# Attention and a mixture of experts on one core: probabilities times values of a query tile in one run

## The chip, the cores and the metric

The kernel runs on one core of one Trainium2 chip. The metric is the time of one execution on the device, in microseconds. The changed kernel is compared with the kernel before on the same inputs.

## The reference

One layer over 2048 tokens of 128 values, in float32. It is causal attention with 8 heads of 64, then a layer norm, a mixture of 16 experts (top 2) with a shared expert, and a second layer norm. The change touches the attention alone:

```
t = tokens * rsqrt(mean(tokens * tokens) + eps) * rms_w
q, k, v = einsum('bnd,hde->bhne', t, wq / wk / wv)
score = where(causal_mask, -max, einsum('bhie,bhje->bhij', q, k) * scale)
out = einsum('bhij,bhje->bhie', softmax(score), v) * sigmoid(t @ w_gates)
pred = einsum('bhne,hed->bnd', out, wo)
x = layernorm(tokens + pred)
```

## The kernel before

The 8 heads are worked on in 4 pairs, the first three in a loop, the last one outside of it. Each engine has its own queue, written by hand, and they wait for each other by semaphores. Within a pair the 2048 queries are 16 tiles of 128, in the order 0, 2, ..., 14, 15, 13, ..., 1 (`ORDER`), and s is the place in that order. The keys of tile t are the key tiles 0 to t, cut into chunks of 512 keys, four key tiles each (`chunks[s]`), of which the last may be narrower.

A query tile goes through four stages, each a step later than the one before:

- `scores` (step s): per head and chunk, TensorE multiplies into one of four PSUM banks ps_s (L1044, L1048 for the mask, L1050). VectorE copies the bank into probs, with the maximum of each row (L755), and after the last chunk reduces the maxima (L761, L762). ScalarE then takes the exponential of the whole row of the head at once, in place (`exps`, L557).
- `turn` (step s + 1): per head and chunk, TensorE transposes the up to four 128x128 blocks into ps_t (L961). There are two such banks, taken in turn by the number g of the group. Groups with an even g are moved to probsT by ScalarE (L568), those with an odd g by VectorE (L771); the moves raise moved0 and moved1. Group g waits until group g - 2 is moved.
- `times_v` (step s + 2): TensorE multiplies the transposed probabilities by v_sb, key tile by key tile and head by head, and adds up in ps_o (L1079): 128x64 weights, 128 columns. In the trace each float32 matmul has two records, so a key tile has four. ScalarE then unloads ps_o into outT (`unload`, L578).
- `times_wo` (step s + 3): TensorE multiplies by the output weights (L1089), and VectorE adds the result to x_acc (L780 to L787), which raises acc_done.

Which unit comes when is set once for all engines by `step_units(s, project)`. Each stage of a step is a list of units. Unit i of a list of n gets the key (i + 0.5) / n, for times_v (i + 0.7) / n, and the units of the step are sorted by it. Before, times_v has one unit per chunk of the tile, so up to four in a step. An engine works its units off in that order; a unit whose wait isn't met holds those behind it.

After the four pairs come the layer norm, the shared expert, the routing and the 16 experts. The change touches none of them.

Of the kernel before, what the change touches and what calls it, by code (L numbers as in the profile page):

```python
# [5 lines left out]
def attention_moe_layer(nc, tokens, wq, wk, wv, wo, w_gates, rms_w, Wg, W1, b1, W11, b11, W2, b2,  # L6
# [12 lines left out]
    P = 128  # L19
# [7 lines left out]
    BT = BANK // P  # L27
# [27 lines left out]
    first = {}  # L55
# [16 lines left out]
    n0, n1, n2, n3 = NORM_ORDER  # L72
    norm_at = {NT: [("stats", n0), ("stats", n1)], NT + 1: [("norm", n0), ("norm", n1), ("stats", n2)]}

    def step_units(s, project):

        units = []
        if s < NT:
            units += [("scores", s, h, c, w) for h in range(2) for c, w in chunks[s]]
        stages = [units]  # L80
        if 1 <= s <= NT:
            stages.append([("turn", s - 1, h, c, w) for h in range(2) for c, w in chunks[s - 1]])
        if 2 <= s < NT + 2:
            stages.append([("times_v", s - 2, 0, c, w) for c, w in chunks[s - 2]])
        if s >= 3:
            stages.append([("times_wo", s - 3, 0, 0, 0)])
        if project:
            stages.append([("project", w, 0, c, 0) for w, c in project_at.get(s, [])])
        else:
            stages.append([(stage, 0, 0, c, 0) for stage, c in norm_at.get(s, [])])  # L90
        placed = [((i + (0.7 if x[0] == "times_v" else 0.5)) / len(u), k, x) for k, u in enumerate(stages) for i, x in enumerate(u)]
        return [x for _, _, x in sorted(placed, key=lambda y: y[:2])]
# [24 lines left out]
    with ctx:  # L117
# [385 lines left out]
        def _(act):  # L503
# [48 lines left out]
            def pair(p, units, fill_of):  # L552
                def exps(s, h):
                    w = (ORDER[s] + 1) * P
                    row = slice(2 * s + h, 2 * s + h + 1)
                    act.wait_ge(row_max, p * (2 * NT) + (2 * s + h + 1))
                    nc.scalar.activation(probs[s % 2][h][:, 0:w], probs[s % 2][h][:, 0:w], ACT.Exp,  # L557
                                         bias=nmax[:, row], scale=SCALE,
                                         accum_out=rsum[:, row]).then_inc(exp_done, 1)

                def move(s, h, c, w):
                    g = first[s, h] + c
                    if g % 2 == 0:
                        if s >= 2:

                            act.wait_ge(pv_done, p * NT + (ONE + s - 1))
                        act.wait_ge(turned, p * GROUPS + (ONE + g + 1))
                        nc.scalar.activation(  # L568
                            probsT[s % 2][h][:, c * BT:c * BT + w // P, :].rearrange("p n i -> p (n i)"),
                            ps_t[0][:, 0:w], ACT.Copy).then_inc(moved0, 1)  # L570

                def unload(s):
                    act.wait_ge(pv_done, p * NT + (ONE + s + 1))

                    act.wait_ge(wo_done, p * NT + (ONE + max(s - 1, 0)))
                    for h in range(2):
                        rows = slice(h * DH, (h + 1) * DH)
                        nc.scalar.activation(outT[s % 2][h][rows, :], ps_o[s % 2][rows, 0:P], ACT.Copy).then_inc(out_ready, 1)  # L578

                for x in units:  # L580
                    stage, s, h, c, w = x
                    if stage == "project":
                        project(x, fill_of[x], p * FILLS + (PROJECTIONS + fill_of[x]), p)
                    elif stage == "scores" and (c, w) == chunks[s][-1]:
                        exps(s, h)
                    elif stage == "turn":
                        move(s, h, c, w)
                    elif stage == "times_v" and (c, w) == chunks[s][-1]:
                        unload(s)
                    elif stage in ("stats", "norm", "turn_x"):  # L590
                        norm(stage, c)
# [367 lines left out]
        def _(pe):  # L959
# [67 lines left out]
            def pair(p, units, fill_of):  # L1027
                def free_bank(n):

                    if n < RING:  # L1030
                        pe.wait_ge(v_ready, p * NC + (n + 1))
                    else:
                        pe.wait_ge(freed, p * FREED + (ONE + KQ_FILLS + n - RING + 1))

                def scores(s, h, c, w, n):
                    t = ORDER[s]
                    if s == 0 and h == 0:

                        pe.wait_ge(freed, p * FREED + (ONE + KQ_FILLS))

                        pe.wait_ge(k_twice, p * (64 * NC) + 64 * NC)
                    free_bank(n)
                    q = q_hl[h][:, t * P:(t + 1) * P]
                    nc.tensor.matmul(ps_s[n % RING][:, 0:w], q, k_h[h][:, c * BANK:c * BANK + w],  # L1044
                                     start=True, stop=False)
                    if c == len(chunks[s]) - 1:

                        nc.tensor.matmul(ps_s[n % RING][:, w - P:w], ident_b[:, :], mask_b[:, :],  # L1048
                                         start=False, stop=False, skip_group_check=True)
                    nc.tensor.matmul(ps_s[n % RING][:, 0:w], q, k_l[h][:, c * BANK:c * BANK + w],  # L1050
                                     start=False, stop=True).then_inc(fill, 1)

                def turn_probs(s, h, c, w):
                    g = first[s, h] + c
                    if c == 0:
                        pe.wait_ge(exp_done, p * (2 * NT) + (2 * s + h + 1))

                    pe.wait_ge((moved0, moved1)[g % 2], p * (GROUPS // 2) + (ONE + g // 2))
                    for j in range(w // P):
                        at = c * BANK + j * P  # L1060
                        mm = turn(ps_t[g % 2][:, j * P:(j + 1) * P], probs[s % 2][h][:, at:at + P])
                    mm.then_inc(turned, 1)

                def times_v(s, c, w):
                    t = ORDER[s]
                    if c == 0:
                        if s == 0:

                            pe.wait_ge(v_ready, p * NC + NC)

                        pe.wait_ge(acc_done, p * NT + (ONE + max(s - 1, 0)))

                    done = first[s, 1] + c + 1
                    pe.wait_ge(moved0, p * (GROUPS // 2) + (ONE + (done + 1) // 2))
                    pe.wait_ge(moved1, p * (GROUPS // 2) + (ONE + done // 2))
                    for j in range(c * BT, c * BT + w // P):
                        for h in range(2):
                            rows = slice(h * DH, (h + 1) * DH)
                            mm = nc.tensor.matmul(ps_o[s % 2][rows, 0:P], v_sb[:, j, rows], probsT[s % 2][h][:, j, :],  # L1079
                                                  start=(j == 0), stop=(j == t))  # L1080
                    if j == t:
                        mm.then_inc(pv_done, 1)

                def times_wo(s):
                    pe.wait_ge(out_ready, p * (2 * NT) + (ONE + 2 * s + 2))
                    if s == 0:
                        pe.wait_ge(pair_wo, p + 1)
                    for h in range(2):
                        mm = nc.tensor.matmul(ps_o[s % 2][:, P + h * D:P + (h + 1) * D], outT[s % 2][h][:, :], wo_p[:, :],  # L1089
                                              start=True, stop=True)  # L1090
                    mm.then_inc(wo_done, 1)

                for x in units:
                    stage, s, h, c, w = x
                    if stage == "project":
                        if high_of.get(x) == 0:

                            pe.wait_ge(pair_w, p * 2 + 2)
                        free_bank(fill_of[x])
                        project(x, fill_of[x], p + 1)  # L1100
                    elif stage == "scores":
                        scores(s, h, c, w, fill_of[x])
                    elif stage == "turn":
                        turn_probs(s, h, c, w)
                    elif stage == "times_v":
                        times_v(s, c, w)
                    elif stage == "times_wo":
                        times_wo(s)
                    elif stage == "turn_x":
                        norm(stage, c)  # L1110
# [127 lines left out]
```

## Time and profile before

| | |
|---|---|
| device time, 3 runs | 773.39 us median, 773.01 to 776.36 |
| profiled execution: span from the first to the last instruction | 773.9 us |
| the profiled execution's own time | no separate number; the span is 0.5 us above the median |
| attention, four pairs | from 34.3 to 566 us of the span |
| TensorE matmul row busy | 688.3 us (89%) |
| VectorE, ScalarE, GpSimd busy | 534.2 us (69%), 419.2 us (54%), 105.3 us (14%) |
| mean granted TensorE clock | 0.947 |

Times are microseconds of one profiled execution. PE is TensorE's matmul row and PEld its weight loads, DVE is VectorE, ACT is ScalarE. The ends of matmuls are modelled and overlap; the distance between starts tells how fast they follow each other.

### The profile page before, as it was taken

How to read it: one execution, taken by the hardware profiler on the slowest of the kernel's cores; microseconds unless marked ns; L12 is line 12 of the kernel's file. 1: busy time of each engine (PE TensorE's matmuls, PEld its weight loads, DVE VectorE, ACT ScalarE, POOL GpSimd, SP SyncE). 2: the span in 40 equal slices, each digit the busy share in tenths (PEclk: the TensorE clock that was granted, in tenths of full speed). 3: DMA queues.
4: the chain of work that ended last, by engine and by line, in shares of the span. 5: the costliest groups of instructions: out<-in, count | busy, mean ns of one | idle time of the engine just before them, and what ended most of it. 6: DMA issues, size and time to landing. Idle time of an engine off the chain costs nothing.

```text
span 773.9 us, 17695 instructions
## 1 busy us (share of the span) xinstructions
PE 688.3 (89%) x5442; PEld 523.0 (68%) x5443; DVE 534.2 (69%) x1874; ACT 419.2 (54%) x908; POOL 105.3 (14%) x172
## 2 busy tenths in 40 slices
PE   4799999979999997999999899999958987999940
PEld 3577777747777774777777577777744556878830
DVE  4687767678777777787767888776787523556536
ACT  4766555656655557655555766554533213454445
POOL 2000000000000000000000000000021773565540
PEclk9999999998999999899999999999976996999975
DMA  8300000040000004000000694000090112222224
GB/s 188 83 2 1 2 3 1 8 107 2 1 2 2 2 1 111 3 1 1 2 2 1 145 130 4 2 2 2 1 302 25 49 52 56 65 63 64 67 73 113
DMA packets 56260, 33.64 MB, mean 43 GB/s; under 512 B 23776, under 2 KB 49520, under 8 KB 56176
## 3 DMA queue, kind: packets, MB, share of 16 engines
q1 hardware_dynamic: 53616, 27.33, 17.6%
q0 software_dynamic: 2560, 5.26, 2.0%
q8 instruction: 44, 0.72, 0.4%
q14 instruction: 40, 0.33, 0.1%
HBM read 14.70 MB, written 9.48 MB: 31 GB/s over the span
## 4 chain that ended last, share of the span: by engine, by line
PE 61%; issue 12%; DVE 12%; POOL 6%; ACT 4%; DMA 3%; SPq 0%; POOLq 0%; DVEq 0%; ACTq 0%
PE ps_o L1079 16%; PE ps_t L961 16%; PE ps_s L1044 9%; PE ps_s L1050 8%; POOL x_sorted L480 4%; PE ps_o L1089 3%; PE ps_s L1193 3%; DVE q_hl L674 2%; PE ps_o L1208 2%; DMA y_rows<-y_sb,row_now 1%; DVE k_l L674 1%; ACT probsT L568 1%; PE ps_s L1048 1%; DVE probs L755 1%; POOL y_rows L490 1%
## 5 line engine op out<-in xcount | busy, mean ns | idle before, releaser
L755 DVE TENSOR_SCALAR_CACHE_REDUCE probs<-ps_s 128x512 f32<-128x512 f32 (+3 forms) x320 | 192.1, 607 | 77.2 <-PE ps_s L1050 75.2
L557 ACT ACTIVATE probs<-probs,nmax 128x128 f32<-128x128 f32 (+15 forms) x128 | 154.0, 1203 | 133.5 <-DVE nmax L762 133.1
L961 PE MATMUL ps_t<-ident,probs 128*128 128x128 f32 x1104 | 181.6, 281 | 17.5 <-ACT probs L529 11.1
L961 PEld LDWEIGHTS ps_t<-ident,probs 128*128 128x128 f32 x1104 | 130.8, 142 | 64.7 <-issue 23.5
L1079 PE MATMUL ps_o<-probsT,v_sb 128*64 128x128 f32 x2176 | 154.4, 280 | 0.0
L1044 PE MATMUL ps_s<-k_h,q_hl 128*128 128x512 f32 (+3 forms) x320 | 145.2, 454 | 6.1 <-issue 5.4
L1079 PEld LDWEIGHTS ps_o<-probsT,v_sb 128*64 128x64 f32 x2176 | 115.7, 137 | 38.6 <-issue 36.1
L1050 PE MATMUL ps_s<-k_l,q_hl 128*128 128x512 f32 (+3 forms) x320 | 128.5, 402 | 0.0
L568 ACT ACTIVATE probsT<-ps_t 128x512 f32<-128x512 f32 (+3 forms) x160 | 89.6, 560 | 62.2 <-PE ps_t L961 60.8
L771 DVE COPY probsT<-ps_t 128x512 f32<-128x512 f32 (+3 forms) x160 | 91.1, 570 | 25.7 <-PE ps_t L961 25.3
L1044 PEld LDWEIGHTS ps_s<-k_h,q_hl 128*128 128x128 f32 x320 | 62.4, 195 | 19.3 <-issue 14.8
L1050 PEld LDWEIGHTS ps_s<-k_l,q_hl 128*128 128x128 f32 x320 | 64.2, 201 | 0.0
L430 POOL COPY wo_p<-wo_sb 128x128 f32 (+1 forms) x4 | 1.2, 293 | 408.1 <-PE ps_o L1089 399.3
L1193 PE MATMUL ps_s<-xgT,w_now 128*128 128x128 f32 x384 | 54.9, 288 | 1.1 <-ACT xgT L617 0.2
L490 POOL DMA_INDIRECT y_rows<-y_sb,row_now x48 | 47.3, 984 | 45.2 <-POOL row_now L486 37.7
L1193 PEld LDWEIGHTS ps_s<-xgT,w_now 128*128 128x128 f32 x384 | 48.3, 198 | 6.5 <-issue 4.4
L922 DVE SCALAR_TENSOR_TENSOR hid<-ps_s,b_col,sil 128x128 f32<-128x128 f32 x96 | 29.2, 346 | 32.1 <-ACT sil L622 26.7
L1089 PE MATMUL ps_o<-wo_p,outT 128*128 128x128 f32 x256 | 41.1, 284 | 6.4 <-ACT outT L578 6.4
L1089 PEld LDWEIGHTS ps_o<-wo_p,outT 128*128 128x128 f32 x256 | 34.7, 194 | 11.5 <-ACT outT L578 7.1
L629 ACT ACTIVATE y_sb<-ps_o 128x128 f32<-128x128 f32 x48 | 13.3, 277 | 50.9 <-DMA y_rows<-y_sb,row_now 47.7
L972 PE MATMUL ps_s<-tT,wkq_p 128*128 128x512 f32 x64 | 35.6, 667 | 2.4 <-DVE tT L696 1.7
L578 ACT ACTIVATE outT<-ps_o 64x128 f32<-64x128 f32 x128 | 34.1, 267 | 5.2 <-PE ps_o L1079 3.4
(150 smaller groups left out, 790.3 us busy)
## 6 DMA issues: line engine op xcount, KB each, us to landing
k_h<-k_h SPq DMA_DIRECT2D x32, 128.0 KB, 2.3
k_l<-k_l SPq DMA_DIRECT2D x32, 128.0 KB, 2.4
w_up<-in_L_ffn_W SPq DMA_DIRECT2D x2, 2048.0 KB, 12.1
xg<-x_sorted SPq DMA_DIRECT2D x48, 64.5 KB, 1.8
x_sorted<-zeros SPq DMA_DIRECT2D x12, 256.0 KB, 9.5
act_s<-y_rows SPq DMA_DIRECT2D x8, 256.0 KB, 4.9
x_acc<-in_L_attn_tokens SPq DMA_DIRECT2D x4, 256.0 KB, 3.6
out<-x_acc SPq DMA_DIRECT2D x4, 256.0 KB, 2.3
```

The source lines that it names most:

```text
L490: nc.gpsimd.indirect_dma_start(out=y_rows, out_offset=bass.IndirectOffsetOnAxis(ap=row_now[:, b:b + 1], axis=0), in_=y_sb[:, b, :], in_off ...
L557: nc.scalar.activation(probs[s % 2][h][:, 0:w], probs[s % 2][h][:, 0:w], ACT.Exp, bias=nmax[:, row], scale=SCALE, accum_out=rsum[:, row]). ...
L568: nc.scalar.activation(probsT[s % 2][h][:, c * BT:c * BT + w // P, :].rearrange("p n i -> p (n i)"), ps_t[0][:, 0:w], ACT.Copy).then_inc(m ...
L755: nc.vector.tensor_scalar(probs[s % 2][h][:, c * BANK:c * BANK + w], ps_s[n % RING][:, 0:w], 1.0, None, ALU.mult, ALU.max, accum_out=cmax[ ...
L771: nc.vector.tensor_copy(probsT[s % 2][h][:, c * BT:c * BT + w // P, :].rearrange("p n i -> p (n i)"), ps_t[1][:, 0:w]).then_inc(moved1, 1)
L961: return nc.tensor.transpose(dst, src, ident[:, :])
L972: mm = nc.tensor.matmul(ps_s[n % RING][:, :], wkq_p[:, w, :], tT[:, c * BANK:(c + 1) * BANK], start=True, stop=True)
L1044: nc.tensor.matmul(ps_s[n % RING][:, 0:w], q, k_h[h][:, c * BANK:c * BANK + w], start=True, stop=False)
L1050: nc.tensor.matmul(ps_s[n % RING][:, 0:w], q, k_l[h][:, c * BANK:c * BANK + w], start=False, stop=True).then_inc(fill, 1)
L1079: mm = nc.tensor.matmul(ps_o[s % 2][rows, 0:P], v_sb[:, j, rows], probsT[s % 2][h][:, j, :], start=(j == 0), stop=(j == t))
L1089: mm = nc.tensor.matmul(ps_o[s % 2][:, P + h * D:P + (h + 1) * D], outT[s % 2][h][:, :], wo_p[:, :], start=True, stop=True)
L1193: mm = nc.tensor.matmul(ps_s[2 * b + a][:, m * P:(m + 1) * P], w_now[:, b, a * H + m * P:a * H + (m + 1) * P], xgT[:, b, :], start=True, s ...
```

## The change

The list of times_v units of a tile has one entry, with all its chunks, where it had one entry per chunk. With one unit, the key of the spread-out order is 0.7 in each step. On TensorE, times_v goes over all key tiles 0 to t in one go. It waits at its start for all moves of the tile, where each unit waited for those of its chunk. ScalarE unloads at the place of the single unit. Work, data, buffers and DMAs are the same.

```diff
+    def pv_groups(s):
+
+        return [(0, len(chunks[s]))]
+
     def step_units(s, project):
...
         if 2 <= s < NT + 2:
-            stages.append([("times_v", s - 2, 0, c, w) for c, w in chunks[s - 2]])
+            stages.append([("times_v", s - 2, 0, c, w) for c, w in pv_groups(s - 2)])
...
-                    elif stage == "times_v" and (c, w) == chunks[s][-1]:
+                    elif stage == "times_v" and (c, w) == pv_groups(s)[-1]:
                         unload(s)
...
-                def times_v(s, c, w):
+                def times_v(s, c, end):
                     t = ORDER[s]
...
-                    done = first[s, 1] + c + 1
+                    done = first[s, 1] + end
                     pe.wait_ge(moved0, p * (GROUPS // 2) + (ONE + (done + 1) // 2))
                     pe.wait_ge(moved1, p * (GROUPS // 2) + (ONE + done // 2))
-                    for j in range(c * BT, c * BT + w // P):
+                    for j in range(c * BT, min(end * BT, t + 1)):
```

## Rows read from the trace of the kernel before

**Rows 1.** The page: busy tenths and granted clock in 40 equal slices of the span.
```profile
PE   4799999979999997999999899999958987999940
...
DVE  4687767678777777787767888776787523556536
...
PEclk9999999998999999899999999999976996999975
```

**Rows 2.** Windows: us; PE, PEld, DVE, ACT, POOL busy (instructions), PEclk, DMA share, GB/s.
```profile
34.30:171.20 136.90, 130.12 (x1120) 98.50 (x1120) 103.36 (x344) 82.15 (x156) 0.85 (x4) 1.00 0.08 17
...
sum 531.70, PE 512.18 PEld 390.48 DVE 401.24 ACT 318.09 POOL 1.97; mean PE 128.04 PEld 97.62 DVE 100.31 ACT 79.52 POOL 0.49
```

**Rows 3.** Timeline, 90 to 96 us: start, duration, engine, operation [idle before <-releaser].
```profile
89.79 0.69 DVE L771 COPY probsT<-ps_t 128x512 f32<-128x512 f32 x1
...
90.39 0.68 DVE L755 TENSOR_SCALAR_CACHE_REDUCE probs<-ps_s 128x512 f32<-128x512 f32 x1
90.41 0.44 PE L1079 MATMUL ps_o<-probsT,v_sb 128*64 128x128 f32 x4
...
90.78 0.49 PE L1044 MATMUL ps_s<-k_h,q_hl 128*128 128x512 f32 x1
...
91.00 0.08 DVE L755 DVE_READ_ACCUMULATOR probs<-ps_s 128x1 f32 x1
...
91.47 0.49 PE L961 MATMUL ps_t<-ident,probs 128*128 128x128 f32 x3
...
91.72 0.48 PE L1044 MATMUL ps_s<-k_h,q_hl 128*128 128x512 f32 x1
...
92.26 0.60 PE L961 MATMUL ps_t<-ident,probs 128*128 128x128 f32 x4
...
92.78 2.00 ACT L557 ACTIVATE probs<-probs,nmax 128x2048 f32<-128x2048 f32 x1 [1.22 <-DVE nmax L762]
...
92.79 1.09 PE L1079 MATMUL ps_o<-probsT,v_sb 128*64 128x128 f32 x16
...
93.81 0.50 PE L1044 MATMUL ps_s<-k_h,q_hl 128*128 128x512 f32 x1
...
94.39 0.60 PE L961 MATMUL ps_t<-ident,probs 128*128 128x128 f32 x4
...
94.74 0.48 PE L1044 MATMUL ps_s<-k_h,q_hl 128*128 128x512 f32 x1
...
94.90 0.60 ACT L568 ACTIVATE probsT<-ps_t 128x512 f32<-128x512 f32 x1
...
95.55 0.66 PE L961 MATMUL ps_t<-ident,probs 128*128 128x128 f32 x4
```

**Rows 4.** Timeline of PE, 80 to 112 us: a run of 12 and the next unit.
```profile
102.54 0.88 PE L1079 MATMUL ps_o<-probsT,v_sb 128*64 128x128 f32 x12
103.35 0.39 PE L1044 MATMUL ps_s<-k_h,q_hl 128*128 128x256 f32 x1
```

**Rows 5.** Waits over the span: who <- for whom: us in total, times, longest.
```profile
PEld ps_o L1079 <- issue: 36.1, 142, 0.8
...
PEld ps_t L961 <- ACT probsT L568: 17.2, 32, 1.2
```

**Rows 6.** Timeline, 47.5 to 57.9 us.
```profile
50.88 0.31 PE L1044 MATMUL ps_s<-k_h,q_hl 128*128 128x128 f32 x1
...
54.28 0.60 ACT L568 ACTIVATE probsT<-ps_t 128x512 f32<-128x512 f32 x1
...
56.37 0.48 PE L1044 MATMUL ps_s<-k_h,q_hl 128*128 128x512 f32 x1
...
57.73 0.33 PE L961 MATMUL ps_t<-ident,probs 128*128 128x128 f32 x1 [0.65 <-ACT probsT L568]
```

**Rows 7.** Timeline of PE at the start of the second pair.
```profile
171.26 0.32 PE L1044 MATMUL ps_s<-k_h,q_hl 128*128 128x128 f32 x1 [2.75 <-issue]
```

**Rows 8.** Windows at the start of the second pair.
```profile
174.00:180.00 6.00, 6.00 (x27) 4.47 (x27) 3.89 (x18) 3.53 (x10) 0.00 (x0) 0.57 0.00 1
```

## The prediction, made before the changed kernel was run

> **What bounds the kernel now.** I read the page first, then the windows of the four head pairs, the order of TensorE's work in a middle step, the list of waits, and the chain behind the longest stall. TensorE's matmul row is busy for 89% of the span, VectorE for 69%, and the granted clock shows 9 tenths nearly everywhere [rows 1]. In the four stretches of attention, together 531.7 us, TensorE is busy for 512.2 us and VectorE for 401.2 us [rows 2]. So in attention TensorE's queue sets the time. A microsecond taken from its stream is gained only if the next instruction isn't then held by ScalarE or VectorE.
>
> **What a run of probabilities times values costs.** A key tile of 128 takes 4 matmul records (two heads, two records each). In [rows 3] I compare start times. A run of 16 records starts 0.53 us after the four transposes before it (92.26 to 92.79), where a score unit starts 0.35 us after such transposes (94.39 to 94.74): 0.18 us is lost on the way in. The next unit starts 1.02 us after a run of 16 and 0.37 us after a run of 4 (90.41 to 90.78), and 0.81 us after one of 12 [rows 4]. That is (1.02 - 0.37) / 12 = 0.054 us a record and 0.155 us beside the records. So each run costs 0.34 us whatever its length, where it stands between transposes and scores (0.32 us between scores and transposes, by the same reading). The waits agree: the weight load of these runs sat idle before 142 of them, 36.1 us in all, with nothing that released it [rows 5].
>
> **What the change removes.** The tile order is 0, 2, ... 14, 15, 13, ... 1. A tile t has t // 4 + 1 runs before and one after, so a pair goes from 4 x (1 + 2 + 3 + 4) = 40 runs to 16. 24 runs x 4 pairs = 96, and 96 x 0.33 = **31.7 us** less on TensorE. The matmuls, their data and the number of turn, score and output units stay. The waits on moved0 and moved1 that the longer run asks for at its start were met a step before: its tile was turned in the previous step. The wait on acc_done is later than before and so free. The semaphore waits that go are inside the 0.33 us. No DMA changes, and GpSimd only waits for wo_done. Bounds of the saving: 24 us, from 36.1 / 142 = 0.25 us a run [rows 5], and 35 us, from 0.36 us a run where the following unit is also slow by 0.02 us.
>
> **What the change moves.** Several units with one fractional key spread over the step: runs stood at 0.175, 0.425, 0.675 and 0.925 of a step. The single one stands at 0.7. So the first 0.7 of a step holds no such run, and the last 0.3 holds up to 64 records, 64 x 0.054 + 0.34 = 3.8 us. What did the runs in the first part hide? The chain is in [rows 3] too: at 90.78 the last score unit of the second head starts, VectorE copies it and takes the maximum, at 92.78 ScalarE starts the exponential of the whole row (2.00 us), and only then, at 94.90, it moves the first turned group of the next step (0.60 us) out of ps_t0. The second group after that needs the same bank, so TensorE can start it only at 95.55: 4.77 us after 90.78. Between lies its own work: masked scores 0.69, transposes of 3 tiles 0.25, scores 0.55, transposes with the way into a run 0.53, **the run 1.02**, scores 0.57, transposes 0.35, scores 0.55, together 4.51. The stall is 0.26 us. After the change the run isn't there: the work is 4.51 - 1.20 = 3.31 and the stall is 4.77 - 3.31 = 1.46 us. The whole run, not only its fixed part, turns into waiting.
>
> I did this sum for each row's second head in a pair: the delay from the last score unit to the end of the first move, read from the traces of the two engines (the first and the longest of the ten, s = 4 and s = 8, are in [rows 3, 6]), plus 0.05 us, less the work that the new order leaves. With step s as place in the tile order (s = 8 is tile 15), delay / work left / stall in us:
> s = 4: 4.05 / 2.70 / 1.35; s = 5: 4.00 / 2.97 / 1.03; s = 6: 3.98 / 2.67 / 1.31; s = 7: 4.43 / 2.97 / 1.46; s = 8: 4.77 / 3.30 / 1.47; s = 9: 4.07 / 2.62 / 1.45; s = 10: 4.32 / 3.15 / 1.17; s = 11: 3.62 / 2.75 / 0.87; s = 12: 3.89 / 3.59 / 0.30; s = 13: 3.19 / 2.51 / 0.68.
> That is 11.1 us a pair. The stalls of the same kind there now add up to 1.9 us a pair; of these the largest, 0.81 us before the transpose at 57.73 (scores at 56.37 take 0.55 us of the 1.36 between the two, [rows 6]; s = 5, first head), goes away, for after the first head's last scores the order now has the long run. The list of waits has 17.2 us in 32 such waits [rows 5], which with some 0.2 us each for a weight load that would have started early anyway is the same amount. At the other places (s = 0 to 3 and 14, 15) the order is the same or the cover suffices. Added: 9.2 x 4 = **36.8 us**.
>
> Two of the delays should shrink. In s = 4 and 6 VectorE was behind when the last, narrow score unit came; after the long run it has caught up. From its instructions (0.61 us a 512-wide score copy, 90.39 to 91.00, and 0.60 us a move, 89.79 to 90.39, [rows 3]) I take 0.2 and 0.25 us off, 1.8 us in four pairs. Against that, transposes that come after a stall or a run take 0.06 us longer to give way, for their weights were not loaded ahead (a difference that I read between the transposes after stalls and the others: 0.59 us to the next run where 0.53 is usual): about 1 us. Added in all: 36.
>
> **Is VectorE then the bound?** A new pair has 16 x 0.34 + 544 records x 0.054 = 34.8 us in long runs. The first pair's 137 us [rows 2] become 137 - 8 + 9 = 138, so 103 us lie between the runs. VectorE has 103.4 us busy in a pair, in 344 instructions, and some 0.03 us between each two: 114 us. So it has to do 11 us of its work inside the runs, 0.7 us in each. It can: when a run starts, it may be behind by a score copy or two and a move, 1.2 to 1.8 us. I add nothing, but the margin is thin, and it makes rival B.
>
> **The sum.** The profiled execution's span is 773.9 us, 0.5 above the median of 773.39. 773.9 - 31.7 + 36 = 778.2, so **778 us** as a median: a change that takes 96 switches off TensorE and gives the same time back as waits for ScalarE.
>
> **The rivals.**
> *A, the saving wins.* The exponential's cover isn't as short as I add up, because TensorE's stall lets VectorE run ahead and the row maximum comes 0.3 us earlier everywhere. Ten stalls x 4 pairs x 0.3 = 12 us less: 766 us. With no new stall at all, 773.9 - 31.7 = 742 us. Against it: the stalls of now sit where this sum puts them, with 0.1 us of error. Chance 0.20.
> *B, VectorE becomes the bound.* It idles in the long run, and what it was behind holds the turn banks or the score banks between the runs. If it did nothing in any run, a pair would take 114 + 34.8 = 149 us instead of 138: 4 x 11 = 44 us more, 822. It decides from where the lag at a run's start falls under the 0.7 us that it needs. If it is three quarters of that, a quarter of the bound is lost: 11 us, 789. Against it: four score banks and two turn banks let TensorE be ahead by more than that. Chance 0.20, with 783 to 800. A rule of the Trainium skill speaks for this side: "Perfetto Trace Analysis", section "Optimization Strategy", advises interleaving stretches that are bound by different engines, which is what the old order does and the new one undoes. By that rule the new order is slower, as in B; this case's trace bears it out so far as the stall without a run is longer by the run.
> *C, the clock falls.* Before 171.26 TensorE had idled for 2.75 us [rows 7], and from 174 to 180 us the granted clock is 0.57, so most of that time at the lower of its two levels, 1.2 of 2.4 GHz [rows 8]: 6 x 0.43 = 2.6 us lost. The point from which it decides: if stalls of 1 us or more are enough, there are seven in each pair, 28 x 2.6 = 73 us, 851 us. Against it: the stall of 0.81 us at 57.73 did not lower it, and between two stalls lie some 10 us of full work. Chance 0.05.
> *D, the change doesn't save what it removes*, because a long run stalls in itself where the short ones ended: 773.9 + 36 = 810 us with nothing saved, 798 with a third. Nothing inside the runs of 16 shows it. Chance 0.03.
>
> **How the numbers follow.** Forecast 0.52, with its own range of 771 to 785 (saving 24 to 35, stalls 32 to 40). The range that should hold it 8 times in 10: from A's 766 to B's 789. A measurement of this kernel tells 0.5%, 3.9 us, from no change; so faster is under 769.5 and slower over 777.3. Of the forecast's 0.52, 0.20 lies above, 0.30 within and 0.02 below. A gives 0.16 faster and 0.04 the same; B, C and D 0.27 slower with 0.01 the same. Together: faster 0.18, same 0.35, slower 0.47.
>
> **What would show it.** 16 runs a pair with 0.054 us a record inside and the weight load's idle time before them down from 36 to some 14 us. Idle time of the transposes for ScalarE's move up from some 20 to 45 to 55 us, in stalls of 0.7 to 1.5 us, once a step, on the second even group. VectorE's waits for scores longer, up to 3 us, once a step, in the long run. The first-head stall at s = 5 gone. Wrong if the stall falls on another engine's wait (VectorE's move, the score banks), if a run's records slow down inside, or if the clock shows dips in the middle of pairs.

## The result: 0.5% slower, and the profile after

The changed kernel takes 777.74 us (median of 20 runs, 774.47 to 781.48), the kernel before in the same comparison 773.42 us (20 runs, 770.83 to 776.80). The ratio is 1.005, with a 95% interval of 1.0033 to 1.0066: 4.3 us slower, 2.6 to 5.1.

The profiled execution of the changed kernel has a span of 774.4 us and took 776.17 us. So some 1.8 us lie around a span, and the profiled execution of before (773.9 us) was about 2 us over its median. Differences between the two traces as wholes are therefore good to some 2 us. I compare the pairs of heads. The windows of the changed kernel, with the columns of [rows 2]:

```profile
32.26:170.40 138.14, 124.88 (x1120) 98.55 (x1121) 102.27 (x344) 81.93 (x157) 1.14 (x5) 1.00 0.08 17
170.40:309.24 138.84, 125.82 (x1121) 99.36 (x1121) 102.33 (x344) 81.70 (x156) 0.82 (x3) 0.98 0.08 17
309.24:445.38 136.14, 126.63 (x1120) 100.37 (x1121) 102.10 (x344) 81.20 (x155) 0.29 (x1) 0.98 0.11 24
```

The three looped pairs take 138.1, 138.8 and 136.1 us; before they took 136.9 [rows 2], 138.8 and 135.2. The fourth, from its first score unit to its last output matmul, takes 129.0 us for 127.7. TensorE is busy for 5 to 7 us less in each looped pair, and the time is the same or a little longer: 3.4 us in the four together. The granted clock of a pair is no lower than before (1.00, 0.98, 0.98 for 1.00, 0.97, 0.98). The second pair hides part of its loss in the clock. In the trace of before it was low for longer at that pair's start: 0.57 in the 6 us from 174 [rows 8], and 0.87 in the 6 us ahead of them:

```profile
168.00:174.00 6.00, 2.77 (x18) 1.97 (x16) 2.50 (x14) 1.58 (x5) 0.53 (x2) 0.87 0.04 11
```

In the changed kernel the same two stretches read:

```profile
168.00:174.00 6.00, 3.22 (x15) 2.44 (x16) 2.34 (x13) 1.87 (x8) 0.16 (x1) 0.78 0.03 8
174.00:180.00 6.00, 5.89 (x40) 4.34 (x38) 5.65 (x27) 4.52 (x12) 0.00 (x0) 0.93 0.01 1
```

By the granted clock that is 3.4 us lost before (6 x 0.13 + 6 x 0.43) and 1.7 us after, so at an equal clock this pair would be over 1 us longer as well.

The waits over the span (columns as in [rows 5]) show what took the place of the work:

```profile
DVE probs L759 <- PE ps_s L1054: 114.7, 99, 4.0
...
PEld ps_t L965 <- ACT probsT L572: 43.0, 46, 1.7
...
PE ps_t L965 <- ACT probsT L572: 27.4, 35, 1.2
...
PEld ps_o L1083 <- issue: 15.9, 53, 0.8
PEld ps_t L965 <- DVE probsT L775: 14.1, 40, 0.7
```

The idle time before the runs' weight loads went from 36.1 to 15.9 us, that of the transposes for ScalarE's move from 17.2 to 43.0 us [rows 5]. And a wait is there that the kernel before did not have, 14.1 us of transposes for VectorE's move. These are idle times of the weight loads, which otherwise run ahead of the matmuls, so TensorE itself loses less: by the starts of its units 34.7 us at the waits for ScalarE's move (10.0 before) and some 6.7 us at those for VectorE's. A long run and the unit after it (TensorE, 106 to 114 us):

```profile
109.08 3.71 PE L1083 MATMUL ps_o<-probsT,v_sb 128*64 128x128 f32 x64
112.72 0.50 PE L1048 MATMUL ps_s<-k_h,q_hl 128*128 128x512 f32 x1
```

The 64 records take 3.64 us from start to start, against 1.02 us for 16 [rows 3]: (3.64 - 1.02) / 48 = 0.055 us a record, with nothing lost inside. The stall of s = 8 in the timeline of the changed kernel, 88 to 98 us, answers to [rows 3]:

```profile
89.19 0.47 PE L1048 MATMUL ps_s<-k_h,q_hl 128*128 128x512 f32 x1
...
91.17 2.01 ACT L561 ACTIVATE probs<-probs,nmax 128x2048 f32<-128x2048 f32 x1 [1.10 <-DVE nmax L766]
...
92.10 0.48 PE L1048 MATMUL ps_s<-k_h,q_hl 128*128 128x512 f32 x1
...
93.17 0.58 ACT L572 ACTIVATE probsT<-ps_t 128x512 f32<-128x512 f32 x1
...
93.80 0.66 PE L965 MATMUL ps_t<-ident,probs 128*128 128x128 f32 x4 [0.98 <-ACT probsT L572]
```

From the last score unit of the second head to the freed transposes it is 93.80 - 89.19 = 4.61 us, where it was 4.77. TensorE used to fill all but 0.26 us of it; now the score unit at 92.10 (0.55 us) is the last thing that it has, and the excess is 1.15 us.

### The profile page after: what moved, and what is told of

Same layout as the page of the kernel before. It is cut to its first block, busy times and chain, and to the rows that moved or that the text cites. A ratio compares the mean times of both kernels' runs of the same rounds, so it can differ in the third digit from the quotient of the medians.

```text
span 774.4 us, 17599 instructions
## 1 busy us (share of the span) xinstructions
PE 663.6 (86%) x5442; PEld 521.6 (67%) x5443; DVE 528.8 (68%) x1874; ACT 417.3 (54%) x908; POOL 105.2 (14%) x172
## 4 chain that ended last, share of the span: by engine, by line
PE 49%; issue 18%; DVE 17%; ACT 7%; POOL 5%; DMA 3%; SPq 1%; DVEq 0%; POOLq 0%; ACTq 0%
PE ps_o L1083 16%; PE ps_t L965 11%; PE ps_s L1048 6%; PE ps_s L1054 5%; POOL x_sorted L484 4%; PE ps_s L1197 3%; ACT probsT L572 3%; DVE probs L759 3%; PE ps_o L1093 3%; DVE q_hl L678 2%; PE ps_o L1212 2%; DVE k_l L678 2%; DMA y_rows<-y_sb,row_now 2%; ACT probs L561 1%; DVE probsT L775 1%
## 5 line engine op out<-in xcount | busy, mean ns | idle before, releaser
L965 PE MATMUL ps_t<-ident,probs 128*128 128x128 f32 x1104 | 179.5, 280 | 42.1 <-ACT probsT L572 27.4
L1083 PE MATMUL ps_o<-probsT,v_sb 128*64 128x128 f32 x2176 | 132.9, 275 | 1.3 <-DVE probsT L775 1.3
L1083 PEld LDWEIGHTS ps_o<-probsT,v_sb 128*64 128x64 f32 x2176 | 117.6, 137 | 17.8 <-issue 15.9
L1093 PEld LDWEIGHTS ps_o<-wo_p,outT 128*128 128x128 f32 x256 | 34.7, 194 | 9.5 <-ACT outT L582 6.5
L484 POOL DMA_INDIRECT x_sorted<-rows,slot x32 | 32.1, 1004 | 25.3 <-DVE slot L867 15.8
```

Of the source, the lines that this page charges most:

```text
L484: nc.gpsimd.indirect_dma_start(out=x_sorted, out_offset=bass.IndirectOffsetOnAxis(ap=slot[:, k, t:t + 1], axis=0), in_=rows[:, k, t, :], i ...
L965: return nc.tensor.transpose(dst, src, ident[:, :])
```

## The experiments

The theory: a run costs 0.33 us of TensorE where it is entered and left, and each step loses the cover of ScalarE's late move. The rivals: the 0.33 us belong to the unit's semaphore waits; VectorE, starved in the long run, is what costs; the saving fills a hole that is there anyway. Ratios are to the kernel before, run on the same chip in turn.

**Four units, back to back.** The kernel before, with all units of a tile at one key:

```diff
-        placed = [((i + (0.7 if x[0] == "times_v" else 0.5)) / len(u), k, x) ...
+        placed = [(0.7 if x[0] == "times_v" else (i + 0.5) / len(u), k, x) ...
```

> The kernel before, with its one unit per 512 keys and all its waits, but all units of a tile with the key 0.7, so that they stand back to back where the changed kernel has its one run. Theory (the 0.33 us a run are paid where TensorE changes between the 64-column weights of these matmuls and the 128-column ones of the others; the loss is ScalarE's late move): the same time as the changed kernel, 777.7 us, within 2 us. Rival (the 0.33 us belong to a unit's own semaphore waits and end): 24 such ends a pair come back, 96 x 0.33 = 32 us more, 810 us; with the waits as half of it, 794 us.

777.01 us, ratio 1.0055 (1.0038 to 1.0072): the changed kernel's time. The waits at the ends of the units cost nothing that can be seen, within some 1.5 us. Its waits are those of the changed kernel:

```profile
PEld ps_t L961 <- ACT probsT L568: 43.6, 47, 1.7
...
PEld ps_o L1079 <- issue: 14.8, 50, 0.8
```

So what a run costs lies at the change to and from the other units, and the effect of the diff is that of the order; what the merged loop adds can't be seen. The Trainium skill, "TensorEngine Tiling (Array Packing)", section "Key Properties", says that changing the tiling mode drains TensorE. This case's trace has a loss at that change: 0.18 us into and 0.155 us out of the 128x64 matmuls, counted from the starts between scores and transposes, both 128x128. That it is a drain, and that the width is the reason, was not tested by itself.

**One run, early.** In the changed kernel:

```diff
+        placed = [(0.2 if x[0] == "times_v" else (i + 0.5) / len(u), k, x) ...
```

> The changed kernel with the key of the single run at 0.2 instead of 0.7 of its step. Theory (ScalarE's late move after the second head's exponential needs a run as cover): the run now stands in that gap, the second head's stalls go (11 us a pair by my sum), and stalls of the first head of 0.2 to 1.3 us come in its place, 7.0 us a pair in all; by the sum of the units a pair takes 2.7 us less than before the change: 773.4 - 11 = 762 us, 757 to 767. Rival (VectorE starves in the long run, wherever it stands): as the changed kernel, 776 to 780 us.

814.42 us, ratio 1.0529 (1.0506 to 1.0552): both sides missed. The waits show one that neither had, and TensorE's timeline where (two runs of short tiles):

```profile
PE ps_o L1083 <- DVE probsT L775: 37.4, 38, 2.6
```

```profile
147.50 1.97 PE L1083 MATMUL ps_o<-probsT,v_sb 128*64 128x128 f32 x32 [1.48 <-DVE probsT L775]
154.36 2.61 PE L1083 MATMUL ps_o<-probsT,v_sb 128*64 128x128 f32 x24 [2.04 <-DVE probsT L775]
```

A single run needs every move of its tile, and the last group is turned at the end of the step before. At 0.2 of a short step that move isn't done, and TensorE's queue stands, 1.48 and 2.04 us in the two rows. In the first pair ten runs wait, 10.0 us together; the pair takes 148.7 us (start to start of the pairs). Before the change the first unit at 0.175 needed only the first chunk's moves. The sum of cover said nothing of this, for it held only one kind of wait.

**Two runs.** Tiles with more than one chunk get two runs, one for each half of the chunks:

```diff
     def pv_groups(s):
-        return [(0, len(chunks[s]))]
+        n = len(chunks[s])
+        return [(0, 1)] if n == 1 else [(0, (n + 1) // 2), ((n + 1) // 2, n)]
...
+        placed = [((0.7 if len(u) == 1 else (0.2, 0.7)[i]) if x[0] == "times_v" else (i + 0.5) / len(u), k, x) ...
```

> The changed kernel with two runs per tile (the halves of its chunks; tiles with one chunk keep one run at 0.7) at the keys 0.2 and 0.7: 28 runs a pair instead of 16 or 40. Theory: 12 x 0.33 = 4 us a pair less than before the change on TensorE, and each half covers one of the two exponentials, so that stalls of 0.3 us a pair are left where the kernel before has 1.8 by the same sum: 5.4 us a pair, 773.4 - 22 = 752 us, 746 to 758. Rival (VectorE starves in long runs): half of the change's loss stays, so 773.4 - 16 + 18 = 775 us.

756.93 us, ratio 0.9781 (0.9758 to 0.9805): 16 to 17 us faster than the kernel before, 5 us short of the forecast of 752 and within its range. The pairs take 132.8, 134.1 and 130.7 us. The waits of the transposes, 36 to 540 us:

```profile
PEld ps_o L1084 <- issue: 25.3, 106, 0.8
...
PEld ps_t L966 <- DVE probsT L776: 8.1, 20, 0.6
...
PEld ps_t L966 <- ACT probsT L573: 7.4, 21, 0.7
```

The 43.0 us of waits for ScalarE's move are down to 7.4. The sum of the units gave 5.4 us a pair, the pairs show 4.1 to 4.7.

> Two runs per tile as before in this study, with the keys 0.25 and 0.65 instead of 0.2 and 0.7. Theory (the cover between exponential and the blocked transposes decides, and the sum of units gives both the same stalls within 0.1 us a pair): 757 us as with 0.2 and 0.7, within 4 us. Rival (the exact place matters through something the sum leaves out, as it did for the single runs at 0.2 and 0.95): off by more than 5 us.

With the keys 0.25 and 0.65: 755.91 us, ratio 0.9777 (0.9740 to 0.9815). Between these two pairs of keys the exact place does not matter. Either version beats both kernels.

**A short exponential.** In the changed kernel and in the one before, the exponential takes the last 128 columns of a row; the other columns stay raw scores and the row's sum is that of the 128:

```diff
-                    nc.scalar.activation(probs[s % 2][h][:, 0:w], probs[s % 2][h][:, 0:w], ACT.Exp,
+                    nc.scalar.activation(probs[s % 2][h][:, w - P:w], probs[s % 2][h][:, w - P:w], ACT.Exp,
```

> The changed kernel with the exponential of a row taken over its last 128 columns alone; the other columns go on as raw scores, and the sum of the row is that of the 128. So ScalarE's instruction takes 0.4 us instead of up to 2.0. Theory (the stall is the length of that instruction): the stalls on ScalarE's move, 9 us a pair in the changed kernel's trace, are gone, about 1 us at a pair's start too: 777.7 - 40 = 738 us, 733 to 745. Rival (VectorE is the bound between the runs): it hardly gains, 765 to 775 us, and the waits of the transposes turn to VectorE's move.

742.52 us, ratio 0.9612 (0.9591 to 0.9634).

> The kernel before, with the exponential of a row over its last 128 columns alone, as in the changed kernel's short-exponential run. Theory: it had only 2 to 3 us a pair of such stalls to lose, so 773 - 8 = 765 us, 760 to 768; and with the stalls gone from both, the distance to the changed kernel with the same edit (742.5) is what the 96 runs cost: 22 to 32 us. Rival (the single place starves VectorE and so costs for itself): the two short-exponential kernels are within 10 us of each other.

760.76 us, ratio 0.9824 (0.9795 to 0.9854). The edit takes 35 us from the changed kernel and 12 to 14 from the one before: the wait for the exponential's end is what the change put in. With it out of both, the fewer runs show a gain, 0.0212 of 773 = 16 us (18 by the medians), less than the 22 to 32 that I expected, and more than the rival's 10. The waits of the changed kernel with the short exponential show what else the change put in:

```profile
PEld ps_t L965 <- DVE probsT L775: 14.1, 40, 0.7
```

It is the same 14.1 us as with the full exponential, so it doesn't come from ScalarE's late move. By the starts of TensorE's units it holds TensorE for 6.7 us here as in the changed kernel. With that the 96 runs come to 23 to 25 us, 0.24 to 0.26 us each. That VectorE falls behind TensorE's denser stream between the runs is likely; no run here tests it.

**One run at 0.8**, the same edit of the key:

> The changed kernel with the key of the single run at 0.8 instead of 0.7, which puts it behind one more score unit. Theory (count of the cover between each exponential and the next transposes of its bank): the second head's stalls stay, and three of the first head's come in addition (s = 5, 11 and 12, 1.0 to 1.3 us, where the run now stands behind the blocked transposes): 3.5 us a pair, 777.5 + 14 = 791 us, 785 to 796. Rival (VectorE's idling in the long run is what costs, wherever it stands): 777 us.

783.85 us, ratio 1.0122 (1.0090 to 1.0153): slower than the changed kernel by some 6 us, and under the expected range of 785 to 796. The direction is the theory's, against a rival that had no change; the size is less than half of its 14 us. The waits show the stalls themselves:

```profile
PEld ps_t L965 <- ACT probsT L572: 54.4, 58, 1.8
```

That is 12 waits more than in the changed kernel, three a pair as expected. In the first pair they hold TensorE for 0.50, 0.39 and 0.86 us, where the sum had 1.0 to 1.3 each.

**One run at 0.95:**

> The changed kernel with the key of the single run at 0.95, the end of its step. The early run at 0.2 lost 10 us a pair in waits for the last move of its own tile, which the step before had only just turned; at 0.95 that move is a step old. Theory: the run covers the second head's exponential, the first head's stalls of 0.3 to 1.3 us come instead (6.7 us a pair by my sum), a pair takes 3.2 us less than before the change: 773 - 13 = 760 us, 755 to 766. Rival (a long run costs through VectorE wherever it stands): 775 to 780 us, or over 800 if the early run's 814 was due to the place in front of the second head's stall.

771.75 us, ratio 0.9967 (0.9951 to 0.9984). Faster than the changed kernel, as the theory has it and the rival hasn't, but 12 us short of the 760 and outside the expected 755 to 766. Reading the starts of units, the first pair's stalls are 0.88 and 0.90 us for the first heads of s = 7 and 8 (0.86 and 0.90 by the sum), but also 1.18 us at s = 4 and 1.0 us before an output unit, which the sum had at nothing: the late run puts off ScalarE's unload, for which the output unit waits and which at s = 4 stands between the exponential and the move.

**Runs of two key tiles.** 72 runs a pair:

```diff
-        return [(0, len(chunks[s]))]
+        n = ORDER[s] + 1
+        return [(j, min(j + 2, n)) for j in range(0, n, 2)]
...
-                    done = first[s, 1] + end
+                    done = first[s, 1] + (end + BT - 1) // BT
...
-                    for j in range(c * BT, min(end * BT, t + 1)):
+                    for j in range(c, end):
```

> The other way round: a run of probabilities times values for every two key tiles, 72 runs a pair instead of 40 or 16, spread over the step as before. Theory (0.33 us a run at the change of the weights' width): 32 x 0.33 = 11 us a pair more, less up to 1.8 us of stalls that the finer spread covers: 773 + 37 to 44 = 810 to 817 us. Rival (the idle time before these weight loads only fills a hole that is there anyway): 775 us.

806.61 us, ratio 1.0401 (1.0368 to 1.0433): 31 us more. There are 128 more units than before, but three in each pair stand right behind another (12 stretches of 16 records in the trace), so TensorE's stream has 276 runs where it had 160. 31 us for 116 runs are 0.27 us each after what the finer spread gained. The stalls on ScalarE's move that it took away were about 7 us in the kernel before, which makes up to 0.33 us a run. The runs cost TensorE time; they fill no hole. The time is 3 us under the expected 810 to 817, which was added up for 128 runs.

**A short accumulation.** The two additions into x_acc take one column instead of 128 (the others are left as they were). VectorE's busy time falls from 528.8 to 512.2 us in the changed kernel, 17 us where I had put it at 26:

```diff
-                        out=x_acc[:, t, :], in0=ps_o[s % 2][:, P:P + D], ...
+                        out=x_acc[:, t, 0:1], in0=ps_o[s % 2][:, P:P + 1], ...
```

> The changed kernel, with the two additions of a step into x_acc over one column instead of 128 (the other columns are left as they were), which takes some 0.4 us of VectorE's work out of each of 64 steps, 26 us in all. Theory (ScalarE's late move is the loss; VectorE has a thin margin): a few of the transposes' new waits on VectorE's move go, 3 to 4 us in attention; the stalls on ScalarE's move stay: 774 us, 770 to 777. Rival (VectorE is the bound between the runs): most of the 26 us come back, 755 to 765 us.

775.18 us, ratio 1.0024 (1.0008 to 1.0040).

> The kernel before with the same edit, for comparison. Theory: VectorE holds nothing there but the two 0.8 us stalls at which the accumulation stands before the score copy: 771 us, 768 to 774. The difference between the two kernels with this edit says how much of the change's loss is VectorE's: none if it stays near 4 us.

771.37 us, ratio 0.9965 (0.9944 to 0.9986). Less work for VectorE is worth 2 to 3 us in either kernel, and the distance between them stays: 3.8 us by the medians, 4.3 with the full accumulation. The time of the changed kernel is the expected one, but not for the expected reason. Its transposes' waits on VectorE's move, of which a few should have gone, are all there:

```profile
PEld ps_t L965 <- DVE probsT L775: 14.1, 40, 0.7
```

What the change loses, it doesn't lose to the accumulations. Whether less work on VectorE between the runs, score copies or moves, would shorten these waits was not tested.

## Why the prediction was right, step by step

The forecast of 778 us and its mechanism held: 96 entries fewer on TensorE, and about the same time back, most of it in waits for ScalarE's move. That the difference of 4.3 us (36 less 31.7) came out to the tenth is luck: the stalls were smaller than added up, VectorE's waits came on top, and the saving is known only as 23 to 32 us.

- **The cost inside a run and at its ends.** Inside, 0.055 us a record was measured for 0.054. The 0.18 and 0.155 us at the ends stand in the new trace as before. As a price in the kernel's time, a run was worth 0.24 to 0.26 us (short exponential) or 0.27 to 0.33 us (runs of two tiles) where I took 0.33. The saving is thus 23 to 32 us, where I predicted 31.7 with bounds of 24 and 35.
- **The stalls.** They are where the sum put them, one a step after the second head's last scores. In the second pair the excess over a unit's usual length, for s = 4 to 13, is 1.08, 0.90, 1.40, 1.30, 1.15, 0.81, 0.96, 0.24, 0 and 0.33 us, against 1.35, 1.03, 1.31, 1.46, 1.47, 1.45, 1.17, 0.87, 0.30 and 0.68. Together 8.2 us for 11.1, with 1.5 us beside them in waits for VectorE's move. Added to the kernel: (9.7 - 1.9) x 4 = 31 us for 36. Two things make the stalls smaller. The delay from the last score unit to the end of the move is 0.13 to 0.29 us shorter than I took it at eight of the ten steps (4.61 for 4.77 at s = 8); taking something off for s = 4 and 6 alone was wrong, and at s = 6 it didn't shrink (4.05 for 3.98). And TensorE takes longer over the work in between than I counted, for part of it waits for VectorE's move. At s = 9 the stretch from the last scores (240.40) to the freed transposes (244.32) holds these rows:

```profile
241.75 0.48 PE L1048 MATMUL ps_s<-k_h,q_hl 128*128 128x512 f32 x1
...
242.55 0.66 PE L965 MATMUL ps_t<-ident,probs 128*128 128x128 f32 x4
242.96 0.48 PE L1048 MATMUL ps_s<-k_h,q_hl 128*128 128x512 f32 x1
...
244.32 0.66 PE L965 MATMUL ps_t<-ident,probs 128*128 128x128 f32 x4 [0.64 <-ACT probsT L572]
```

The score unit at 241.75 takes 0.80 us to the next transposes instead of 0.55, because their bank waits for VectorE: 0.25 us of the stall only changed its name. The stall at the first head of s = 5 is gone, as said.
- **The run's own wait.** I said that its moves were met a step before. In the changed kernel this cost little, 1.3 us of matmul idle time in all; the early run at 0.2 shows that it depends on the place.
- **The balance.** 31 less 23 to 32 gives -1 to 8 us; the four pairs show 3.4 us in the traces, the runs 4.3 us. The rest is within what two traces can tell. My start of 773.9 us was a span and the result a time of the device, which is 1.8 us more; that execution was also 2 us slower than usual, so the mixture put the start only 0.5 us too high.
- **Rival A**, cover longer than counted, is true in part: the stalls are 0.3 us shorter on average, of which 0.13 us by an earlier exponential. It is not enough against the stalls that stay. **Rival B**, VectorE the bound, isn't what happened in the main: ScalarE's waits hold TensorE for 25 us more than before, VectorE's for 6.7 us, and the short accumulation closes none of the gap. But its wait exists, 14.1 us of weight-load idle time in 40 places where I "add nothing". Its 6.7 us are more than the 4.3 us of loss; but without it part of them would come back in longer waits for ScalarE, as the row of s = 9 shows. The rule of the Trainium skill ("Perfetto Trace Analysis", "Optimization Strategy": interleave stretches with different bounds) has the sign right, 1.005; but one piece for each exponential is enough, where the kernel before has one for each 512 keys: the two runs show it with 0.978. **Rival C**, the clock, didn't come: 0.98 to 1.00 in the pairs, with stalls up to 1.4 us. **Rival D** neither: nothing stalls inside 64 records.

## What to carry to other kernels

Work that costs something to enter should come in as few pieces as there are waits to cover, and each piece should be put into the gap between an instruction that starts a long chain on another engine and the first instruction that is held by the chain's end. To find it, add up the durations between the two in the order of issue, once for each wait. Then look at what the moved piece itself waits for: a merged piece needs all its inputs at its start. The same work was 5% slower than before as one piece at 0.2 of its step, and 2% faster as two halves at 0.2 and 0.7. The sum gave the direction in three places (0.8, 0.95 and the two halves) and the time to 5 us for the halves alone; it was 7 us off at 0.8, 12 us at 0.95, and 52 us at 0.2, where the piece's own inputs were left out.

## What was not expected of the hardware

A switch between these 128x64 matmuls and 128x128 ones costs TensorE some 0.3 us in and out, as much as five or six of the records themselves. And stalls of 0.8 to 1.4 us, seven in each pair, left the granted clock of the pairs at 0.98 to 1.00. The 2.75 us before a pair's first unit, after a stretch in which TensorE was busy for 5.95 of 8 us, came with 0.57 in the 6 us from 174 [rows 7, 8]. In the changed kernel 2.95 us of the same kind came with 0.78 and then 0.93 in the two stretches shown above.
